# A graph attention layer and a routed expert layer on one core: four instruction streams reordered, a register kept, two banks alternated

## The chip, the core and the metric

One core of a Trainium2 chip runs the whole kernel in one launch. The metric is the time of one execution on the device in microseconds; the number for a kernel is the median of its runs.

## The reference

`x` is 4096 x 256 in fp32, `adj` a symmetric 0/1 matrix of 4096 x 4096. The layer is a graph attention followed by a mixture of eight experts (two per row), each with a residual:

```python
xn = layernorm(x)
Wh = xn @ W
e  = leaky_relu(Wh @ a[:256] + (Wh @ a[256:]).T, 0.2)
e  = where(adj > 0 or diagonal, e, -9e15)
x  = x + softmax(e, axis=1) @ Wh
xt = layernorm(x)
probs = softmax(xt @ Wr + br)
top_p, top_idx = top_k(probs, 2); weights = top_p / top_p.sum()
xe = layernorm(xt) * ln_g[e] + ln_b[e]
y  = gelu(xe @ W1[e] + b1[e]) @ W2[e] + b2[e]
out = x + sum of the two chosen y, times their weights
```

## The kernel before

Five engine programs are written out by hand and meet in semaphores; nothing is scheduled by a tool. What stands in an engine's program is what it does, in that order.

**Head** (0 to 63 us). VectorE takes statistics of 32 row tiles of x (`next_stats`, `moments`), GpSimd turns variances into reciprocal roots (`scales`), VectorE and GpSimd normalise the tiles, TensorE transposes them in pairs and multiplies by `W` (`pair_t`, `pair_row`, `project`).

**Attention** (63 to 579 us). Step i treats row tile i against all 4096 columns. ScalarE masks the two halves of tile i + 2 (L966) and takes the exponentials of tile i + 1, also in two halves (L1021). TensorE transposes the probabilities in four groups (L776); ScalarE copies each group from PSUM (`p_hi`, L1029: the high parts of three groups and an fp32 copy of the fourth), VectorE makes the low parts (L1314); TensorE multiplies by `Wh` (`av`). Groups 0 and 2 share one PSUM buffer, 1 and 3 the other, so the transposes of group 1 of the next step wait for the copy of group 3. VectorE also makes the scores of tile i + 2 in halves (L1294) and adds mask and minimum (L1302). GpSimd and ScalarE split the expert weights on the side, one chunk a step: a subtraction (L559) and a scaling (`w_scaled`, L1050).

Four finished tiles are a router batch b, treated in the steps that follow; q is i modulo 4. At q = 1 ScalarE normalises the four tiles to rows (`normalise`, L1037); at q = 2 TensorE transposes them (L808), ScalarE copies (L1056), TensorE forms the logits (L819); at q = 3 VectorE finds the two experts and their one-hots (L1382 to L1386) and TensorE counts positions (`router_pos`, L827 to L831); at q = 0 VectorE reads them (`choose_rows`).

SP's queue runs in this order each step (`tile_step`): store a finished tile (L419), load the two halves of the next adjacency tile (L394, each when ScalarE has masked the half before), store and load weight chunks (L405, L401), load a tile of x again (L426). The last one waits for rows:

```python
def load_x1(n):
    if n >= XRING:
        sp.wait_ge(s_row, n - XRING + 1)
        sp.wait_ge(s_out, 16 * (n - XRING + 2))
    sp.dma_start(x1[n % XRING][:, :], x_view[:, n, :]).then_inc(s_xr[n % XRING], 16)
```

**Experts** (579 us to the end). 32 full tiles of 256 rows and 7 half tiles of 128 (from NB = 32 to FT = 39), each of one expert, whose number is read from a table at run time. For tile t TensorE does `up` of t + 1 (L901 to L903), the transposes of t + 2 (L879) and `down` of t (L919, L922) into the PSUM banks `acc`; VectorE splits x and h and forms the result (L1609 to L1617), GpSimd scatters it with an add into `out` (L665), one scatter after the other has landed. The first 12 tiles and those from 28 on are written out, the rest is a loop.

Of the kernel before, what the change touches and what calls it, by code (L numbers as in the profile page):

```python
# [22 lines left out]
def build(nc, x, adj, gnn_w, gnn_a, w_r, b_r, ln_g, ln_b, w1, b1, w2, b2, out):  # L23
# [61 lines left out]
    with ExitStack() as ctx:  # L85
# [253 lines left out]
        def halves(t):  # L339

            return S if not isinstance(t, int) or t < NB else 1

        def total(t, each):

# [349 lines left out]
        def _(pe):  # L694
# [139 lines left out]
            def attend(i):  # L834

                u, b, q = i % 2, i // RB - 1, i % RB
                now = i < T
                if now:
                    p_transpose(i, u, 0)
                    if i == 0:  # L840
                        project(NP - 1)
                    p_transpose(i, u, 1)
                if i > 0:
                    av(i - 1, 1 - u, 2)
                    av(i - 1, 1 - u, 3)
                if in_batch(b) and q == 2:
                    router_t(b, 0)
                if now:
                    p_transpose(i, u, 2)
                    av(i, u, 0)  # L850
                if in_batch(b) and q == 2:
                    router_mm(b, 0)
                    router_t(b, 1)
                if in_batch(b) and q == 3:
                    router_pos(b)
                if now:
                    p_transpose(i, u, 3)
                    av(i, u, 1)
                if in_batch(b) and q == 2:
                    router_mm(b, 1)  # L860

# [21 lines left out]
            def expert_of(t):  # L883
                return pe.value_load(table_e[0:1, bass.ds(t, 1)], min_val=0, max_val=E - 1)

            def up(t, first=0, last=HC):
                e = expert_of(t)
                if first == 0:
                    pe.wait_ge(s_wr, e * CHUNKS + CHUNKS)
                    pe.wait_ge(s_xh, t + 1)  # L890
# [14 lines left out]
                        m.then_inc(s_g1, 1)  # L905

            def down(t, u):
                e = expert_of(t)
                pe.wait_ge(s_hh, t + 1)
                if within(t, 1, FT):  # L910
                    pe.wait_ge(s_yc, total(t, 2))
                else:
                    pe.wait_ge(s_x1, X1 * (T - 1) + 3)
                ns = halves(t)
                for c in range(HC):
                    w_both = w_blocks[:, bass.ds(e * CHUNKS + 2 + c // 4, 1), :, (c % 4) * D:(c % 4 + 1) * D].rearrange("p a z n -> p (a z) n")
                    w_hi = w_both[:, 0, :]
                    for s in range(ns):
                        pe.matmul(acc[s][:, :], h_hi[u][:, (c * ns + s) * P:(c * ns + s + 1) * P], w_both,  # L919
                                  start=(c == 0), stop=False, skip_group_check=True)  # L920
                    for s in range(ns):
                        m = pe.matmul(acc[s][:, 0:D], h_lo[u][:, (c * ns + s) * P:(c * ns + s + 1) * P], w_hi,  # L922
                                      start=False, stop=(c == HC - 1), skip_group_check=True)
                m.then_inc(s_down, 1)

# [33 lines left out]
        def _(act):  # L959
# [129 lines left out]
            def attend(i):  # L1089
# [13 lines left out]
                if i < T - 1:  # L1103
                    exps(i + 1, 1 - u, 0)
                    exps(i + 1, 1 - u, 1)
                if in_batch(b) and q == 1:
                    for k in range(RB):
                        normalise(b, k)
                if in_batch(b) and q == 2:
                    router(b, 0)  # L1110
                if now:
                    p_hi(i, 2)
                    w_scaled(i)
                if ahead:
                    mask(i + 2, u, 1)
                if in_batch(b) and q == 2:
                    router(b, 1)
                if now:
                    p_hi(i, 3)
                if i == T - 2:  # L1120
                    load_first()
                if in_batch(b) and q == 3:
# [79 lines left out]
        def _(dve):  # L1202
# [36 lines left out]

            next_stats(0, 4)  # L1240
            moments(0)
            next_stats(4, 8)
            moments(1)
            scaled_by(0)
            for i in range(4):
                normalise(i)
            next_stats(8, 12)
            scaled_by(1)
            normalise(4)
# [350 lines left out]
            def result(t, r):  # L1600

                e = dve.value_load(table_e[0:1, bass.ds(t, 1)], min_val=0, max_val=E - 1)
                ns = halves(t)
                y = y_sb[r % 2]
                dve.wait_ge(s_down, t + 1)
                if within(t, 2, FT):
                    dve.wait_ge(s_ysc, total(t - 1, 16))
                for s in range(ns):
                    dve.scalar_tensor_tensor(out=y[:, s, :], in0=acc[s][:, D:2 * D], scalar=1.0 / LOSCALE,  # L1609
                                             in1=b2_rep[:, bass.ds(e * D, D)], op0=ALU.mult, op1=ALU.add).then_inc(s_yc, 1)  # L1610
                dve.wait_ge(s_yc, total(t, 2) + ns)
                for s in range(ns):
                    dve.tensor_tensor(y[:, s, :], acc[s][:, 0:D], y[:, s, :], ALU.add).then_inc(s_yc, 1)
                dve.wait_ge(s_yc, total(t + 1, 2))
                dve.wait_ge(s_wt, t + 1)
                for s in range(ns):
                    ins = dve.tensor_scalar(y[:, s, :], y[:, s, :], weight[r][:, s:s + 1], None, ALU.mult)  # L1617
                ins.then_inc(s_y, 1)
# [68 lines left out]
```

## Time and profile before

| | us |
|---|---|
| median of 3 runs | 990.39 |
| range of the runs | 988.03 to 991.64 |
| profiled execution | 994.33 |
| its span | 992.4 |
| TensorE busy | 950.7 |
| VectorE busy | 788.8 |
| ScalarE busy | 615.4 |
| GpSimd busy | 622.0 |

The profiled execution is one run of its own; sums are made against it. In the rows PE is TensorE's matmuls, PEld its weight loads, DVE VectorE, ACT ScalarE, POOL GpSimd, SPq SP's DMA issues; L12 is a line of the kernel. Ends of matmuls are modelled, so idle time of PE is counted from a modelled end, some 0.16 us after the array is free for a transpose. What released a wait is inferred from semaphores. A wait named "issue" is one for nothing that the profile shows.

### The profile page before, as it was taken

What the parts mean: (1) busy time and instruction counts of PE and PEld (TensorE: products, weight loads), DVE (VectorE), ACT (ScalarE), POOL (GpSimd) and SP (SyncE); (2) the same over time, 40 slices, a digit from 0 to 9 for tenths busy, and PEclk for the clock granted to TensorE, in tenths of its full rate; (3) what the DMA queues carried; (4) which work ended last, traced back from release to release, by engine and by line L of the source; (5) the groups of instructions that cost most, each with busy time, mean ns of one, the idle gap of its engine ahead of it and who ended that gap; (6) DMA issues with size and microseconds to landing.
All of it is one profiled execution on the core that took longest, in us unless ns stands there. A gap on an engine that the chain in (4) does not pass through costs nothing. (4 is left out here: it accounts for less than half of the span.)

```text
span 992.4 us, 22974 instructions
## 1 busy us (share of the span) xinstructions
PE 950.7 (96%) x7562; PEld 799.7 (81%) x7563; DVE 788.8 (79%) x1199; ACT 615.4 (62%) x905; POOL 622.0 (63%) x630
## 2 busy tenths in 40 slices
PE   6999999999999999999999999999999999999994
PEld 5788999989988889888888977777777777777762
DVE  6789989999999999999999446787666666577653
ACT  4889898788888887878786554433333433333441
POOL 5221251486674964847629458888888888888652
PEclk9999999999999999999999999999999999999998
DMA  8658878688787787886877986443332332232321
GB/s 265 134 159 254 269 237 272 205 256 242 223 260 271 221 258 244 236 270 181 264 240 202 352 336 212 94 110 62 61 55 44 48 58 43 43 52 46 44 35 22
DMA packets 92636, 170.71 MB, mean 172 GB/s; under 512 B 20480, under 2 KB 69888, under 8 KB 84224
## 3 DMA queue, kind: packets, MB, share of 16 engines
q1 hardware_dynamic: 57984, 133.54, 40.3%
q0 software_dynamic: 24048, 26.23, 17.0%
q10 hardware_dynamic: 10512, 9.72, 3.4%
q8 instruction: 57, 0.93, 0.4%
q14 instruction: 35, 0.29, 0.1%
HBM read 136.65 MB, written 41.19 MB: 179 GB/s over the span
## 5 line engine op out<-in xcount | busy, mean ns | idle before, releaser
L1162 ACT ACTIVATE hf<-tp,b_cols 128x256 f32<-128x256 f32 (+1 forms) x312 | 116.4, 460 | 176.1 <-PE tp L903 173.7
L795 PE MATMUL acc<-wh,pt_hi 128*128 128x256 f16 x768 | 209.3, 273 | 0.0
L796 PE MATMUL acc<-wh,pt_hi 128*128 128x256 f16 x768 | 209.3, 273 | 0.0
L797 PE MATMUL acc<-wh,pt_lo 128*128 128x256 f16 x768 | 209.3, 273 | 0.0
L559 POOL TENSOR_TENSOR x_late<-x_late,wsp 128x1024 f32<-128x1024 f32 x32 | 78.9, 2464 | 178.2 <-DMA x_late<-in_L_ffn_W 173.0
L919 PE MATMUL acc<-w_sb,h_hi 128*128 x568 | 170.9, 379 | 5.1 <-issue 3.8
L1294 DVE SCALAR_TENSOR_TENSOR sc<-t_row,s_col 128x2048 f32<-128x2048 f32 x64 | 166.4, 2599 | 9.1 <-PE tp L776 6.9
L901 PE MATMUL tp<-x_hi,w_sb 128*128 128x256 f16 (+1 forms) x624 | 161.2, 264 | 1.9 <-ACT hf L1162 1.8
L665 POOL DMA_INDIRECT out<-y_sb,yidx x71 | 120.9, 1703 | 65.2 <-DVE y_sb L1617 38.1
L903 PE MATMUL tp<-x_down,w_sb 128*128 128x256 f16 (+1 forms) x624 | 161.2, 264 | 0.0
L902 PE MATMUL tp<-x_lo,w_sb 128*128 128x256 f16 (+1 forms) x624 | 160.8, 263 | 0.0
L1021 ACT ACTIVATE sc<-sc,mn 128x2048 f32<-128x2048 f32 x64 | 127.8, 2000 | 27.0 <-DVE mn L1302 26.9
L1302 DVE CUSTOM_DVE_ANT_0 sc<-sc,bias_sb 128x4096 f32<-128x4096 f32 x32 | 141.6, 4425 | 1.6 <-issue 0.2
L776 PE MATMUL tp<-ident,sc 128*128 128x128 f32 x1024 | 129.9, 274 | 9.4 <-ACT pt L1029 6.7
L599 POOL DMA_INDIRECT rows_dram<-rows,slot x64 | 118.0, 1844 | 23.2 <-issue 16.6
L1314 DVE SCALAR_TENSOR_TENSOR pt_lo<-tp,pt_hi 128x1024 f16<-128x1024 f32 x96 | 113.9, 1207 | 21.6 <-ACT pt_hi L1029 11.2
L1029 ACT ACTIVATE pt_hi<-tp 128x1024 f16<-128x1024 f32 x96 | 95.1, 1017 | 54.7 <-PE tp L776 50.0
L776 PEld LDWEIGHTS tp<-ident,sc 128*128 128x128 f32 x1024 | 114.6, 141 | 16.9 <-ACT pt L1029 8.3
L966 ACT ACTIVATE bias_sb<-adj_sb,big 128x2048 bf16<-128x2048 f32 x64 | 127.9, 1999 | 0.0
L1586 DVE CAST x_hi<-xg 128x512 f16<-128x512 f32 (+1 forms) x39 | 19.8, 508 | 123.9 <-ACT xg L1151 110.2
L799 PE MATMUL acc<-wh,pt 128*128 128x256 f32 x512 | 115.8, 379 | 0.0
L922 PE MATMUL acc<-w_sb,h_lo 128*128 x568 | 113.0, 273 | 0.0
(238 smaller groups left out, 1779.4 us busy)
## 6 DMA issues: line engine op xcount, KB each, us to landing
adj_sb<-in_adj SPq DMA_DIRECT2D x64, 1024.0 KB, 7.5
x_late<-in_L_ffn_W SPq DMA_DIRECT2D x32, 512.0 KB, 9.8
wsplit_dram<-wsp SPq DMA_DIRECT2D x32, 512.0 KB, 7.3
w_sb<-wsplit_dram SPq DMA_DIRECT2D x32, 512.0 KB, 8.7
xs<-rows_dram ACTq DMA_DIRECT2D x32, 260.0 KB, 3.4
wsp<-in_L_ffn_W POOLq DMA_DIRECT2D x32, 256.0 KB, 4.9
x<-in_x SPq DMA_DIRECT2D x32, 128.0 KB, 10.5
out<-x SPq DMA_DIRECT2D x32, 128.0 KB
```

The source lines that it names most:

```text
L776: m = pe.transpose(tp[g % 2][:, c * P:(c + 1) * P], sc[u][:, (GJ * g + c) * P:(GJ * g + c + 1) * P], ident[:, :])
L795: pe.matmul(o, pt_hi[g][:, cols], wh[:, j, 0, :], start=(j == 0), stop=False)
L796: pe.matmul(o, pt_hi[g][:, cols], wh[:, j, 1, :], start=False, stop=False)
L797: m = pe.matmul(o, pt_lo[g][:, cols], wh[:, j, 0, :], start=False, stop=False)
L901: pe.matmul(o, w_hi, x_hi[:, cols], start=(k == 0), stop=False)
L902: pe.matmul(o, w_hi, x_lo[:, cols], start=False, stop=False)
L903: m = pe.matmul(o, w_lo, x_down[:, cols], start=False, stop=(k == KD - 1))
L919: pe.matmul(acc[s][:, :], h_hi[u][:, (c * ns + s) * P:(c * ns + s + 1) * P], w_both, start=(c == 0), stop=False, skip_group_check=True)
L966: act.activation(bias_sb[u][:, cols], adj_sb[:, cols], ACT.Relu, bias=big[:, 0:1], scale=-3.0e38).then_inc(s_mk[h], 1)
L1021: act.activation(sc[u][:, cols], sc[u][:, cols], ACT.Exp, bias=mn[u][:, 0:1], scale=-1.0, accum_out=rsum[u][:, h:h + 1]).then_inc(s_e[h], 1)
L1294: dve.scalar_tensor_tensor(out=sc[u][:, cols], in0=t_row[:, cols], scalar=s_col8[:, bass.ds(n, 1)], in1=t2_row[:, cols], op0=ALU.add, op1= ...
L1302: dve.tensor_tensor_reduce(sc[u][:, :], sc[u][:, :], bias_sb[u][:, :], 1.0, 3.0e38, ALU.add, ALU.min, mn[u][:, 0:1]).then_inc(s_b, 1)
```

## The change

- VectorE, head: rows 0 and 1 are normalised right after the first four tiles' moments, ahead of the next four tiles' statistics.
- TensorE: `router_pos` goes behind the fourth group's transposes and the second product group of its step.
- ScalarE: `w_scaled` of each step, and the four rows of a q = 1 step, go behind the copy of the fourth group.
- TensorE, experts: where t is known when the program is written, `up` keeps the expert's register and `down` uses it.
- TensorE and VectorE, half tiles: odd and even tiles use different banks of `acc`, and `down` waits for the result two tiles back.

```diff
+        def bank_of(t):
+            return (t - NB) % 2 if isinstance(t, int) and t >= NB else 0
...
-                if in_batch(b) and q == 3:
-                    router_pos(b)
                 if now:
                     p_transpose(i, u, 3)
                     av(i, u, 1)
+                if in_batch(b) and q == 3:
+                    router_pos(b)
...
+            experts = {}
+
             def up(t, first=0, last=HC):
-                e = expert_of(t)
+                e = experts[t] if first > 0 else expert_of(t)
+                if isinstance(t, int):
+                    experts[t] = e
...
             def down(t, u):
-                e = expert_of(t)
+                e = experts.pop(t) if isinstance(t, int) and t in experts else expert_of(t)
+                a = bank_of(t)
                 pe.wait_ge(s_hh, t + 1)
-                if within(t, 1, FT):
+                if within(t, NB + 1, FT) and isinstance(t, int):
+                    pe.wait_ge(s_yc, total(t - 1, 2))
+                elif within(t, 1, FT):
                     pe.wait_ge(s_yc, total(t, 2))
...
-                        pe.matmul(acc[s][:, :], h_hi[u][:, (c * ns + s) * P:(c * ns + s + 1) * P], w_both,
+                        pe.matmul(acc[s + a][:, :], h_hi[u][:, (c * ns + s) * P:(c * ns + s + 1) * P], w_both,
...
-                if in_batch(b) and q == 1:
-                    for k in range(RB):
-                        normalise(b, k)
                 if in_batch(b) and q == 2:
                     router(b, 0)
                 if now:
                     p_hi(i, 2)
-                    w_scaled(i)
                 if ahead:
                     mask(i + 2, u, 1)
                 if in_batch(b) and q == 2:
                     router(b, 1)
                 if now:
                     p_hi(i, 3)
+                    w_scaled(i)
+                if in_batch(b) and q == 1:
+                    for k in range(RB):
+                        normalise(b, k)
...
             next_stats(0, 4)
             moments(0)
+            scaled_by(0)
+            normalise(0)
+            normalise(1)
             next_stats(4, 8)
             moments(1)
-            scaled_by(0)
-            for i in range(4):
-                normalise(i)
+            normalise(2)
+            normalise(3)
```

VectorE's `result` reads `acc[s + a]` in the same way.

On ScalarE, in step 5 (q = 1), the first with a router batch: `sc,rsum` are the exponentials, `rows` the normalised rows, `pt_hi` and `pt` the copies, `wsp` the scaling, `bias_sb` the mask. Before:

```order
L1021 ACTIVATE sc,rsum<-sc,mn 128x2048 [waits masked_with_min_done]
L1021 ACTIVATE sc,rsum<-sc,mn 128x2048
L1037 ACTIVATE rows<-x_0,nb,rs 128x256 [waits row_shift_done]
L1037 ACTIVATE rows<-x_1,nb,rs 128x256 [waits row_shift_done]
L1037 ACTIVATE rows<-x_2,nb,rs 128x256 [waits row_shift_done]
L1037 ACTIVATE rows<-x_3,nb,rs 128x256 [waits row_shift_done]
L1029 ACTIVATE pt_hi<-tp 128x1024 [waits av_done,p_transposed]
L1050 ACTIVATE wsp<-x_late 128x1024 [waits w_chunk_rest_done]
L966 ACTIVATE bias_sb<-adj_sb,big 128x2048 [waits masked_with_min_done,adj_half_loaded1]
L1029 ACTIVATE pt<-tp 128x1024 [waits av_done,p_transposed]
```

And with the change:

```order
L1032 ACTIVATE sc,rsum<-sc,mn 128x2048 [waits masked_with_min_done]
L1032 ACTIVATE sc,rsum<-sc,mn 128x2048
L1040 ACTIVATE pt_hi<-tp 128x1024 [waits av_done,p_transposed]
L977 ACTIVATE bias_sb<-adj_sb,big 128x2048 [waits masked_with_min_done,adj_half_loaded1]
L1040 ACTIVATE pt<-tp 128x1024 [waits av_done,p_transposed]
L1061 ACTIVATE wsp<-x_late 128x1024 [waits w_chunk_rest_done]
L1048 ACTIVATE rows<-x_0,nb,rs 128x256 [waits row_shift_done]
L1048 ACTIVATE rows<-x_1,nb,rs 128x256 [waits row_shift_done]
L1048 ACTIVATE rows<-x_2,nb,rs 128x256 [waits row_shift_done]
L1048 ACTIVATE rows<-x_3,nb,rs 128x256 [waits row_shift_done]
```

Third copy, mask and fourth copy now come right after the exponentials; scaling and rows come last.

On TensorE, before the down product of a half tile: the transposes of the tile after next, the register load and two register operations, and the product's first instruction with its waits. Before:

```order
L879 MATMUL xt_ps<-ident,xs 128x128 [waits ffn_xt_scaled,xs_loaded0]
L879 MATMUL xt_ps<-ident,xs 128x128
L884 TENSOR_LOAD table_e
L884 ISA x2
L919 ISA [waits ffn_y_low_added,ffn_hidden_split]
L919 MATMUL acc<-w_sb,h_hi 128x512
L922 MATMUL acc<-w_sb,h_lo 128x256
```

And with the change:

```order
L883 MATMUL xt_ps<-ident,xs 128x128 [waits ffn_xt_scaled,xs_loaded0]
L883 MATMUL xt_ps<-ident,xs 128x128
L930 ISA [waits ffn_y_low_added,ffn_hidden_split]
L930 MATMUL acc<-w_sb,h_hi 128x512
L933 MATMUL acc<-w_sb,h_lo 128x256
```

The load and the two register operations are gone there; the waits stay with the product's first instruction.

## Rows read from the trace of the kernel before

**Rows 1.** The page: busy time of the engines (share, instructions), and the group of scores

```profile
PE 950.7 (96%) x7562; PEld 799.7 (81%) x7563; DVE 788.8 (79%) x1199; ACT 615.4 (62%) x905; POOL 622.0 (63%) x630
...
L1294 DVE SCALAR_TENSOR_TENSOR sc<-t_row,s_col 128x2048 f32<-128x2048 f32 x64 | 166.4, 2599 | 9.1 <-PE tp L776 6.9
```

**Rows 2.** Waits, whole span: engine line waited for: us in total, times, longest

```profile
PE tp L776 <- ACT pt L1029: 6.7, 7, 1.3
...
PE rt_ps L827 <- DVE oh L1386: 4.9, 6, 1.2
...
PE acc L919 <- issue: 3.8, 7, 0.7
...
PE tp L776 <- DVE pt_lo L1314: 2.6, 8, 0.9
```

**Rows 3.** Windows, steps 21 to 24: length; busy PE, PEld, DVE, ACT, POOL; PEclk, DMA, GB/s

```profile
423.94:440.50 16.56, 15.41 (x136) 13.87 (x136) 16.36 (x30) 12.77 (x12) 8.99 (x5) 1.00 0.81 259
...
sum 65.49, PE 62.82 PEld 56.85 DVE 62.90 ACT 53.42 POOL 42.21; mean PE 15.70 PEld 14.21 DVE 15.73 ACT 13.36 POOL 10.55
```

**Rows 4.** Timeline, DVE and POOL: start, length, engine, line, operation, [idle before <-releaser]

```profile
372.89 2.35 DVE L1294 SCALAR_TENSOR_TENSOR sc<-t_row,s_col 128x2048 f32<-128x2048 f32 x1 [0.17 <-PE tp L776]
...
403.27 1.23 DVE L1314 SCALAR_TENSOR_TENSOR pt_lo<-tp,pt_hi 128x1024 f16<-128x1024 f32 x1 [1.36 <-issue]
404.41 4.34 DVE L1294 SCALAR_TENSOR_TENSOR sc<-t_row,s_col 128x2048 f32<-128x2048 f32 x1
...
404.43 2.16 POOL L559 TENSOR_TENSOR x_late<-x_late,wsp 128x1024 f32<-128x1024 f32 x1
```

**Rows 5.** Timeline, ScalarE, step 21 (q = 1) and the one behind it

```profile
396.29 2.00 ACT L1021 ACTIVATE sc<-sc,mn 128x2048 f32<-128x2048 f32 x1 [1.56 <-DVE mn L1302]
...
400.27 2.06 ACT L1037 ACTIVATE rows<-x,nb,rs 128x256 f32<-128x256 f32 x4
...
404.09 1.99 ACT L966 ACTIVATE bias_sb<-adj_sb,big 128x2048 bf16<-128x2048 f32 x1
405.99 1.00 ACT L1029 ACTIVATE pt<-tp 128x1024 f32<-128x1024 f32 x1
...
409.09 1.99 ACT L966 ACTIVATE bias_sb<-adj_sb,big 128x2048 bf16<-128x2048 f32 x1
...
417.51 0.57 ACT L1056 ACTIVATE xnt_b<-xt_ps 128x512 f32<-128x512 f32 x1
```

**Rows 6.** Timeline, PE, steps 21 and 22

```profile
407.04 1.09 PE L776 MATMUL tp<-ident,sc 128*128 128x128 f32 x8 [1.33 <-ACT pt L1029]
...
418.35 0.96 PE L819 MATMUL rt_ps<-w_r_sb,xnt_b 128*128 128x8 f32 x8
```

**Rows 7.** Timeline, SP's queue, step 21

```profile
400.88 0.33 SPq L426 DMA_DIRECT2D x<-in_x  x1
...
402.15 4.29 SPq L394 DMA_DIRECT2D adj_sb<-in_adj  x2
```

**Rows 8.** One tile, adj_sb: its transfers

```profile
DMA to landing us min/median/max: 5.8/7.5/11.7
```

**Rows 9.** One line (L884), PEld's queue: us of one, from to; and PEld's timeline, tail

```profile
L884 PEldq TENSOR_LOAD <-table_e x79: 295/303/782, 575.5 to 975.3; - x79
L884 PEldq SEQ_ASSERT  x79: 18/18/26, 576.3 to 976.1; - x79
...
946.15 0.10 PEld L919 LDWEIGHTS acc<-w_sb,h_hi 128*128 128x128 f16 x1 [0.78 <-issue]
```

**Rows 10.** Timeline, PE and POOL, the last tile

```profile
978.42 0.39 PE L919 MATMUL acc<-w_sb,h_hi 128*128 x1 [1.30 <-DVE y_sb L1613]
...
983.87 1.56 POOL L665 DMA_INDIRECT out<-y_sb,yidx  x1 [2.98 <-DMA out<-y_sb,yidx]
```

**Rows 11.** Timeline, PE, head

```profile
10.62 1.11 PE L720 MATMUL tp<-ident,rows 128*128 128x128 f32 x4 [2.07 <-DVE rows L1221]
...
30.99 0.63 PE L720 MATMUL tp<-ident,rows 128*128 128x128 f32 x4 [0.33 <-DVE sc L1221]
```

More of the change, by code:

```diff
@@ L918, in down @@
                     for s in range(ns):
-                        pe.matmul(acc[s][:, :], h_hi[u][:, (c * ns + s) * P:(c * ns + s + 1) * P], w_both,
+                        pe.matmul(acc[s + a][:, :], h_hi[u][:, (c * ns + s) * P:(c * ns + s + 1) * P], w_both,
                                   start=(c == 0), stop=False, skip_group_check=True)
                     for s in range(ns):
-                        m = pe.matmul(acc[s][:, 0:D], h_lo[u][:, (c * ns + s) * P:(c * ns + s + 1) * P], w_hi,
+                        m = pe.matmul(acc[s + a][:, 0:D], h_lo[u][:, (c * ns + s) * P:(c * ns + s + 1) * P], w_hi,
                                       start=False, stop=(c == HC - 1), skip_group_check=True)
@@ L1603, in result @@
                 ns = halves(t)
+                a = bank_of(t)
                 y = y_sb[r % 2]
@@ L1608, in result @@
                 for s in range(ns):
-                    dve.scalar_tensor_tensor(out=y[:, s, :], in0=acc[s][:, D:2 * D], scalar=1.0 / LOSCALE,
+                    dve.scalar_tensor_tensor(out=y[:, s, :], in0=acc[s + a][:, D:2 * D], scalar=1.0 / LOSCALE,
                                              in1=b2_rep[:, bass.ds(e * D, D)], op0=ALU.mult, op1=ALU.add).then_inc(s_yc, 1)
@@ L1612, in result @@
                 for s in range(ns):
-                    dve.tensor_tensor(y[:, s, :], acc[s][:, 0:D], y[:, s, :], ALU.add).then_inc(s_yc, 1)
+                    dve.tensor_tensor(y[:, s, :], acc[s + a][:, 0:D], y[:, s, :], ALU.add).then_inc(s_yc, 1)
                 dve.wait_ge(s_yc, total(t + 1, 2))
```

## The prediction

> **What bounds the kernel now.** TensorE first: it is busy for 950.7 of 992.4 us [rows 1], so only its stalls can be won. The list of its waits, read next, says where they are [rows 2]: seven for ScalarE's copy of the fourth group (6.7 us), six for the one-hots (4.9), eight for VectorE's low parts (2.6), all in the attention, and seven "issue" stalls before the down products (3.8).
>
> Then the four windows of one router batch, steps 21 to 24 (q = 1, 2, 3, 0) [rows 3]. TensorE idles for 2.7 of their 65.49 us, so this looks like TensorE's kernel. But VectorE is busy for 62.90 us of them, no less than TensorE's 62.82. The two run in lock step: a stall taken from TensorE is won only if idle time of VectorE goes with it. VectorE's timeline shows how little it has [rows 4]: 1.36 us before a low part that waited for the copy of the third group (the q = 1 steps but the first have it), and 0.17 before scores that waited for TensorE's fourth transposes in the third step.
>
> **The move on ScalarE, at first sight.** In a q = 1 step the exponentials end at 400.27. Four rows (2.06 us), the third copy and the weight scaling (together to 404.09) and a mask (1.9) stand ahead of the fourth copy at 405.99 [rows 5], which TensorE's next transposes await until 407.04 [rows 6]. With rows and scaling behind it, that copy starts at 403.1 and TensorE's wait is gone; the third copy starts at 400.3, and VectorE's 1.36 us are gone too. If that were all, each batch would be 1.4 us shorter.
>
> **What is queued behind the rows.** Completion of the first row lets SP load an x tile (`load_x1` waits for row n - 5), and behind that load, in SP's order, stands the load of an adjacency half. SP sits until 400.88, just after the first row, and issues the half at 402.15 [rows 7], 1.9 us after the row's start. ScalarE masks the half at 409.09 and hadn't to wait for it [rows 5], so it took at most 6.9 us; the shortest load of the trace took 5.8 [rows 8]. That is about 1 us of slack, and the change moves the first row by two copies and the scaling (1.85 for copy and scaling, 0.9 for the other copy) and the mask (1.9): 4.65 us. The mask of the q = 2 step will wait for its DMA, and with it all that ScalarE has behind it.
>
> How far that reaches, counted from the start of the q = 1 exponentials: exponentials 4.0, copy 0.9, mask 1.9, copy 0.9, scaling 0.95 make 8.65; from row to load issue 1.6 (1.9 here, less where SP's store goes quicker); the load, L; then mask 2.0, two exponentials 4.0 and the router's copy 0.6, before TensorE may start the logits product. Together 16.85 + L. Now the same stretch is 396.29 to 418.35, 22.1 us [rows 5, 6]. With L = 5.8 the new one is 0.55 longer, with 6.9 it is 1.65 longer, with the median of 7.5 [rows 8] 2.25. I take L = 6.3: only two x tiles stand ahead of this half in its queue, which puts it near the minimum. That is +1.05 a batch, and from the logits product on, the fourth transposes, the scores and VectorE's saturated stretch follow as they do now. It occurs six times (q = 1 of steps 5 to 25): **+6.3 us**, bounds +3.3 and +13.5. VectorE's 1.36 us are lost inside this chain, which starts before them.
>
> The Trainium skill (DMA: Bandwidth & Descriptors, Anatomy of one DMA) prices a transfer at about 2.0 us plus bytes over 436 GB/s, an estimate of 4.4 us for this half. By that estimate the six batches would give 5 us back instead; the shortest load here, 5.8, speaks against it, and the sum doesn't use it.
>
> **The other parts.**
> - Step 29 is a q = 1 step with no mask left to load for. Its gain is real: VectorE's 1.36 us, up to the 1.8 that TensorE stalls there. **-1.5**.
> - Step 1: only the scaling moves behind the fourth copy. One of the seven waits [rows 2] is there, and the scaling is 0.95 us of it; VectorE isn't saturated yet. **-1.0**, bounds 0 and -1.0.
> - Position products (L827 to L831) behind the fourth transposes and a product group: TensorE comes to them 3.5 us later than now and finds the one-hots ready, so 4.9 us of waits go [rows 2]. VectorE still has all its work in the same order and wins only where it waited for those transposes: 0.17 once [rows 4], some more in others. **-0.9**, bounds 0 and -4.9; I stand near zero because VectorE is busy for 16.36 of the 16.56 us of this very step [rows 3]. `choose_rows` reads the positions in the next step and isn't held up.
> - Kept register. In the tail (half tiles) TensorE's sequencer has no lead. Before a down product it loads the expert from the table (303 ns) and works on it until the assertion, from 975.3 to 976.1 [rows 9], and the weight loads stand for 0.78 us [rows 9]. There are seven such places, the tiles from 31 on but the last; I take 0.67 each, between 0.3 (the load alone) and 0.78. **-4.7**, bounds -2.1 and -5.5. In full tiles no such wait shows, and nothing is won. The chain that ends last runs through the tail, so it counts in full. What would be late next is VectorE's split of the next x; no wait for it is in [rows 2].
> - Alternating banks: `down` then waits for the result before the previous one. Only the last tile waits for that now, 1.30 us [rows 10]. But the last scatter, at 983.87, waits for the one before it to land, not for its data [rows 10]. **0**, bounds 0 and -0.4.
> - Head: rows 0 and 1 normalised before the second statistics. TensorE can start some 1.6 us before 10.62 [rows 11]. Then it meets VectorE, whose work is neither less nor earlier: at 30.99 it already waits for it [rows 11]. **0**, bounds +0.1 and -1.6.
>
> **Sum**: 6.3 - 1.5 - 1.0 - 0.9 - 4.7 = -1.8 us. The profiled execution took 994.33 (span 992.4), 3.9 above the median of the runs; its own time would become 992.5, and the median of 990.39 becomes **988.6**. About 0.5%, 5 us, is what a measurement of this kernel tells from no change: the forecast is no change, two sides that nearly cancel.
>
> **Rivals.**
> - *The late mask costs nothing*: something covers the logits product, and six batches keep VectorE's 1.36: -8.2 in place of +6.3, sum -16.3, 974. For: no wait of that product is in [rows 2]. Against: the copy that it reads ends within 0.3 us of its start (417.51 + 0.57 against 418.35 [rows 5, 6]). Chance 0.17.
> - *VectorE and GpSimd stand in each other's way less.* At 404.41 scores take 4.34 us, while GpSimd's subtraction runs from 404.43 for 2.16 [rows 4]; all 64 scores average 2.60 us [rows 1] where an undisturbed one takes 2.35 [rows 4], 16 us in all. The change moves their phases. In q = 1 steps the scores would start first, at 403.1, but except in step 29 that falls inside the chain that waits for the mask. In other steps a shift of either sign is open; a third of the 16 us won is -6, sum -7.8, 982.6. Chance 0.13. The Trainium skill (SBUF — State Buffer, SBUF: two separate sides) has the rule that whichever of the two starts first holds the shared ports for its whole instruction; by that rule step 29 gains 2 us more for VectorE, and the sum there goes to the 1.8 of TensorE.
> - *Slower: the half lands late.* Now it is alone in its queue for 4 us; afterwards the second half, free long before, is issued right behind it. If the two share, L is somewhere between 5.8 and the longest load, 11.7 [rows 8]; halfway, 8.8, costs 2.5 us more in six batches, sum +13.2, 1003.6. It decides from L = 7.4 on, where the sum passes +5. For: no row here shows a half with another right behind it and the queue empty. Against: the 6.9 of the half that was issued with a store beside it. Chance 0.12.
> - *The register load isn't what the tail waits for*, and its stalls stay with the semaphores: sum +2.9, 993.3. Chance 0.06.
>
> The forecast has 0.52; of it 0.07 lies below 985.4 and 0.01 above 995.4. With the rivals: **faster 0.31, same 0.57, slower 0.12**. The range for 8 in 10 is **979 to 995**: it takes in the lesser contention and the load up to 7.4, and leaves out the first and the third rival. The forecast's own is 985 to 993.
>
> **What would show it.** In step 21's place the half is issued some 4.7 us later against the exponentials, and the q = 2 mask waits for adj_sb, six times 3 to 4 us. Of TensorE's waits those for the fourth copy and the one-hots are gone; in their place, six times, stands one of the logits product (L819) for the router's copy, 2 to 3 us. The "issue" stalls of the tail are near zero, its tiles 0.7 us closer together. The last scatter still waits for the one before. The forecast falls if L819 doesn't wait, if VectorE's idle time in a batch is under 1 us, or if the tail's stalls only change their name.

## The result, and the profile after

| | before | changed |
|---|---|---|
| median, us | 991.9 (8 runs) | 1000.44 (8 runs) |
| range | 988.03 to 994.30 | 998.73 to 1003.85 |
| profiled execution, its span | 994.33, 992.4 | 999.58, 997.6 |

The ratio is 1.0094 (95% interval 1.008 to 1.0108): slower by 0.9%, 9 us, and outside the range. The forecast was 988.6. The profiled executions are only 5.2 us apart in span: that of before, 994.33, lies at the upper end of its kernel's runs, that of the change, 999.58, near the lower end of its own. So places are found in the traces, and sizes are judged by the ratios.

In the account below, "the minimum" is VectorE's instruction that adds the mask and finds the minimum, "the subtraction" is GpSimd's on the expert weights, and two instructions "meet" when they run at the same time. Busy times and two of VectorE's groups on the page after (scores, and the minimum):

```profile
PE 956.7 (96%) x7562; PEld 803.7 (81%) x7563; DVE 794.6 (80%) x1199; ACT 615.3 (62%) x905; POOL 631.9 (63%) x630
...
L1307 DVE SCALAR_TENSOR_TENSOR sc<-t_row,s_col 128x2048 f32<-128x2048 f32 x64 | 164.0, 2562 | 8.7 <-PE tp L780 6.7
...
L1315 DVE CUSTOM_DVE_ANT_0 sc<-sc,bias_sb 128x4096 f32<-128x4096 f32 x32 | 154.4, 4825 | 1.6 <-issue 0.2
```

VectorE is 5.8 us busier than in [rows 1]. The scores lost 2.4 us, but the minimum took 4.42 us every time before (32 times, 141.6 us), and here it takes 12.8 more in all.

The waits (engine, tile and line waited for; us in total, times, longest):

```profile
ACT bias_sb L977 <- DMA adj_sb<-in_adj: 22.4, 6, 3.9
...
PE rt_ps L823 <- ACT xnt_b L1067: 8.7, 6, 1.7
PE tp L780 <- DVE pt_lo L1327: 7.9, 14, 1.1
```

The waits for the fourth copy and for the one-hots of [rows 2] are gone, as forecast. In their place stand six waits of the mask for the adjacency tile, 3.7 us on average (forecast 3 to 4), and six of the logits product for the router's copy, as forecast, but of 0.8 to 1.7 us and not 2 to 3. The windows of steps 21 to 24, as in [rows 3]:

```profile
396.84:412.05 15.21, 15.02 (x120) 13.49 (x121) 15.09 (x14) 12.15 (x11) 13.86 (x14) 1.00 0.50 147
412.05:433.81 21.76, 19.46 (x146) 17.25 (x145) 18.73 (x17) 15.91 (x18) 13.86 (x8) 0.92 0.93 283
433.81:449.01 15.20, 15.20 (x136) 13.91 (x136) 15.06 (x30) 12.77 (x12) 10.88 (x6) 1.00 0.81 244
449.01:463.86 14.85, 14.85 (x127) 13.57 (x124) 14.61 (x22) 12.58 (x11) 3.28 (x4) 1.00 0.76 248
sum 67.02, PE 64.54 PEld 58.23 DVE 63.49 ACT 53.41 POOL 41.88; mean PE 16.13 PEld 14.56 DVE 15.87 ACT 13.35 POOL 10.47
```

The batch takes 67.02 us, was 65.49: the q = 3 step is 1.36 shorter, the q = 2 step 2.46 longer, and in that step TensorE is *busy* for 1.68 us more with the same work. Its clock column says why: 0.92. Inside it:

```profile
426.46:427.84 1.38, 1.38 (x12) 1.38 (x13) 0.50 (x1) 1.38 (x2) 0.00 (x0) 1.00 1.05 371
427.84:431.30 3.46, 3.46 (x19) 2.91 (x18) 2.25 (x2) 3.38 (x4) 2.19 (x2) 0.51 1.10 385
431.30:433.80 2.50, 2.50 (x25) 2.33 (x24) 2.45 (x4) 0.44 (x1) 2.19 (x2) 1.00 0.86 249
```

For 3.46 us behind the wait of the logits product the granted clock is 0.51, the lower of its two levels (1.2 in place of 2.4 GHz). It happens in three of the six batches (from 294.7, 359.6 and 427.9 us, 3.4 us each); before the tail the trace of before has no such stretch. The Trainium skill ("TensorE: Matmul & The Clock Gate", What's actually happening) knows these two states and no level between; the trace agrees: products of 256 columns stand 109 ns apart at one level and 213 at the other. The length of the wait alone doesn't say whether the clock falls: the two longest waits of the logits product, 1.7 and 1.6 us in the first two batches, are followed by no such stretch, those of 1.6, 1.6 and 1.4 in the next three are.

The chain that was forecast, on ScalarE in steps 21 and 22 (the exponentials, the fourth copy, the rows, the mask, the router's copy), on SP's queue (x load, adjacency half, weight chunk), and on TensorE (logits, then the fourth transposes), in three views:

```profile
403.73 2.00 ACT L1032 ACTIVATE sc<-sc,mn 128x2048 f32<-128x2048 f32 x1 [1.96 <-DVE mn L1315]
...
410.51 1.01 ACT L1040 ACTIVATE pt<-tp 128x1024 f32<-128x1024 f32 x1
...
412.37 2.07 ACT L1048 ACTIVATE rows<-x,nb,rs 128x256 f32<-128x256 f32 x4
...
419.95 2.00 ACT L977 ACTIVATE bias_sb<-adj_sb,big 128x2048 bf16<-128x2048 f32 x1 [3.69 <-DMA adj_sb<-in_adj]
...
425.83 0.57 ACT L1067 ACTIVATE xnt_b<-xt_ps 128x512 f32<-128x512 f32 x1
```

```profile
412.99 0.33 SPq L430 DMA_DIRECT2D x<-in_x  x1
...
413.83 0.93 SPq L398 DMA_DIRECT2D adj_sb<-in_adj  x2
...
415.30 0.43 SPq L405 DMA_DIRECT2D x_late<-in_L_ffn_W  x1
```

```profile
426.46 1.06 PE L823 MATMUL rt_ps<-w_r_sb,xnt_b 128*128 128x8 f32 x8 [1.41 <-ACT xnt_b L1067]
...
427.84 1.89 PE L780 MATMUL tp<-ident,sc 128*128 128x128 f32 x8
```

The first row comes 8.64 us after the start of the exponentials (forecast 8.65), the half is issued 1.46 after it (1.6) and is there after 6.1 (6.3; 5.4 to 6.4 in the six batches, 6.0 on average); the logits product starts 22.73 after the exponentials, where it started 22.06 [rows 5, 6].

What was not forecast is on VectorE and GpSimd in step 22:

```profile
413.03 6.98 DVE L1315 CUSTOM_DVE_ANT_0 sc<-sc,bias_sb 128x4096 f32<-128x4096 f32 x1
...
429.77 3.61 DVE L1307 SCALAR_TENSOR_TENSOR sc<-t_row,s_col 128x2048 f32<-128x2048 f32 x1 [1.21 <-PE tp L780]
...
413.58 2.14 POOL L563 TENSOR_TENSOR x_late<-x_late,wsp 128x1024 f32<-128x1024 f32 x1
...
429.12 2.12 POOL L563 TENSOR_TENSOR x_late<-x_late,wsp 128x1024 f32<-128x1024 f32 x1 [6.96 <-DMA x_late<-in_L_ffn_W]
```

The second scores, 2.35 us before, take 3.61 beside GpSimd's subtraction. It runs there because its weight chunk is loaded behind the late adjacency half (issued at 415.30) and, as seen against the kernel with the rows put back (below), also takes longer: from the start of the exponentials to its issue 11.6 us for 9.8, from issue to subtraction 13.8 for 10.3. In the batches' q = 2 steps these scores take 2.35, 4.03, 3.51, 3.24, 3.61 and 4.23 us. The scores of q = 1 steps that took 4.34 [rows 4] take 2.34 now, but there the mask's wait covers them.

The Trainium skill ("SBUF — State Buffer", SBUF: two separate sides) lets whichever of VectorE and GpSimd starts first keep the shared ports for its whole instruction. The scores at 429.77 agree (second to start, 1.26 longer). The minimum doesn't: VectorE's 6.98 us, 2.56 more than usual, began at 413.03, and the subtraction at 413.58. Nor do the scores of [rows 4], which began 0.02 us ahead of the subtraction and took 4.34, while in the same trace scores at 173.13, 0.05 ahead, kept their 2.33 and the subtraction took 4.28. So the recorded starts alone don't tell which of the two waits; what does is open.

The tail, two of four half tiles of each kernel and the sum over the four, before:

```profile
939.10:946.20 7.10, 6.51 (x67) 4.78 (x68) 3.95 (x8) 3.16 (x12) 5.18 (x8) 1.00 0.42 58
946.20:953.10 6.90, 6.41 (x66) 4.76 (x67) 3.95 (x8) 2.99 (x11) 5.27 (x9) 1.00 0.24 38
...
sum 28.40, PE 26.25 PEld 19.29 DVE 15.87 ACT 12.48 POOL 17.83; mean PE 6.56 PEld 4.82 DVE 3.97 ACT 3.12 POOL 4.46
```

and after:

```profile
945.37:952.22 6.85, 6.79 (x69) 5.00 (x68) 4.00 (x8) 3.09 (x10) 4.76 (x7) 1.00 0.42 58
952.22:958.93 6.71, 6.71 (x68) 4.94 (x67) 3.95 (x8) 3.10 (x10) 4.97 (x7) 1.00 0.26 42
...
sum 27.31, PE 27.24 PEld 20.02 DVE 15.95 ACT 12.38 POOL 19.10; mean PE 6.81 PEld 5.00 DVE 3.99 ACT 3.09 POOL 4.77
```

The "issue" stalls before the down products are gone, but a tile is only 0.3 us shorter: TensorE's busy time rose from 26.25 to 27.24 in these four. In `up` the first products follow each other 56 ns apart, the later ones some 83 on average (every third one 124, the others 60 to 65); before, the first 21 to 24 of 48 went at 56, now 10 do (gaps of one tile's products in the two timelines). That TensorE's sequencer has lost its lead there is the likely reason, but no row shows it. The time won at the load is mostly given back there. The last scatter waits for the one before it as in [rows 10]:

```profile
989.09 1.56 POOL L669 DMA_INDIRECT out<-y_sb,yidx  x1 [3.07 <-DMA out<-y_sb,yidx]
```

### The profile page after: what moved, and what is told of

It is laid out like the page before. It is cut to its first block and busy times, and to the rows that moved or that the text cites. A ratio compares the mean times of both kernels' runs of the same rounds, so it can differ in the third digit from the quotient of the medians.

```text
span 997.6 us, 22905 instructions
## 1 busy us (share of the span) xinstructions
PE 956.7 (96%) x7562; PEld 803.7 (81%) x7563; DVE 794.6 (80%) x1199; ACT 615.3 (62%) x905; POOL 631.9 (63%) x630
## 5 line engine op out<-in xcount | busy, mean ns | idle before, releaser
L563 POOL TENSOR_TENSOR x_late<-x_late,wsp 128x1024 f32<-128x1024 f32 x32 | 83.5, 2610 | 175.7 <-DMA x_late<-in_L_ffn_W 169.2
L1307 DVE SCALAR_TENSOR_TENSOR sc<-t_row,s_col 128x2048 f32<-128x2048 f32 x64 | 164.0, 2562 | 8.7 <-PE tp L780 6.7
L1315 DVE CUSTOM_DVE_ANT_0 sc<-sc,bias_sb 128x4096 f32<-128x4096 f32 x32 | 154.4, 4825 | 1.6 <-issue 0.2
L977 ACT ACTIVATE bias_sb<-adj_sb,big 128x2048 bf16<-128x2048 f32 x64 | 128.0, 2000 | 22.4 <-DMA adj_sb<-in_adj 22.4
```

Of the source, the lines that this page charges most:

```text
L977: act.activation(bias_sb[u][:, cols], adj_sb[:, cols], ACT.Relu, bias=big[:, 0:1], scale=-3.0e38).then_inc(s_mk[h], 1)
L1307: dve.scalar_tensor_tensor(out=sc[u][:, cols], in0=t_row[:, cols], scalar=s_col8[:, bass.ds(n, 1)], in1=t2_row[:, cols], op0=ALU.add, op1= ...
L1315: dve.tensor_tensor_reduce(sc[u][:, :], sc[u][:, :], bias_sb[u][:, :], 1.0, 3.0e38, ALU.add, ALU.min, mn[u][:, 0:1]).then_inc(s_b, 1)
```

## The experiments

"Rows back" below means the changed kernel with the rows where they were. To place differences, six batches are cut at two points that the timelines show: from the start of the exponentials in a q = 1 step to the logits product of the next step (A), and from there to the next q = 1 step's exponentials (B). Each row is read from one trace, and that alone moves B by some 2.5 us, as before and "register alone" show, whose attention is the same. Sums over six batches, us:

| kernel | A | B | stretches at half clock |
|---|---|---|---|
| before | 132.95 | 257.31 | 0 |
| changed | 137.41 | 262.91 | 3 |
| rows back | 132.95 | 253.23 | 0 |
| rows alone | 138.82 | 263.95 | 4 |
| x load a tile later | 127.88 | 254.12 | 0 |
| filler of 14 / of 8 | 139.96 / 139.46 | 259.57 / 261.80 | 0 / 1 |
| positions alone | 132.92 | 257.29 | 0 |
| scaling alone | 132.95 | 251.81 | 0 |
| register alone | 132.94 | 254.81 | 0 |
| short subtraction, changed | 147.04 | 254.48 | 4, three of them 6.8 us |
| short subtraction, rows back | 130.62 | 242.76 | 0 |

### Rows back

```diff
+                if in_batch(b) and q == 1:
+                    for k in range(RB):
+                        normalise(b, k)
                 if in_batch(b) and q == 2:
                     router(b, 0)
...
                     w_scaled(i)
-                if in_batch(b) and q == 1:
-                    for k in range(RB):
-                        normalise(b, k)
```

> The changed kernel with the four rows of a q = 1 step back ahead of the third copy; everything else as changed. Theory A (the rows delay the load of the adjacency half; the q = 2 mask waits, TensorE waits at the logits product, and its granted clock falls to half three times behind such a wait): these batches cost 10.1 us of the two profiles' difference, so this kernel comes out near 987, some 5 us under the kernel before: what stays is step 1 (-1.0), the tail (-2.6), the head (-0.4) and a little from the positions. Theory B (the cost comes from the position products or the scaling in their new places, or from VectorE's minimum meeting GpSimd's subtraction, 12.8 us more in that group): it stays at 995 or above. A also says: no wait for adj_sb in the list of waits, no stretch at half clock before the tail.

Measured 986.99 (5 runs), ratio to before 0.9958 (0.9944 to 0.9971): theory A to the microsecond. The windows of its steps 21 to 24, the sum:

```profile
sum 64.29, PE 62.78 PEld 56.93 DVE 61.76 ACT 53.38 POOL 44.88; mean PE 15.69 PEld 14.23 DVE 15.44 ACT 13.35 POOL 11.22
```

and its wait for the half:

```profile
ACT bias_sb L977 <- DMA adj_sb<-in_adj: 0.3, 1, 0.3
```

The move of the rows is worth +13.5 us (1.0094 - 0.9958 of 991); everything else in the change makes it 4 us faster. In the table the rows are +4.5 in A and +9.7 in B, less 0.9 in steps 29 and 30.

### Rows alone

```diff
-                if in_batch(b) and q == 1:
-                    for k in range(RB):
-                        normalise(b, k)
...
                 if now:
                     p_hi(i, 3)
+                if in_batch(b) and q == 1:
+                    for k in range(RB):
+                        normalise(b, k)
```

> The kernel before with one edit: the four rows of a q = 1 step behind the fourth group's copy. Theory A: the delay of the first row is the same 4.65 us as in the changed kernel, so the six batches cost about 10 us and step 29 gives back 1: some 1001, six waits of the mask for adj_sb of 3 to 4 us, six waits of the logits product, and some stretches at half clock. Theory B: within 3 us of the kernel before.

Measured 1006.98 (5 runs), ratio 1.0174 (1.0154 to 1.0194): 17 us, more than the 10 expected.

```profile
ACT bias_sb L966 <- DMA adj_sb<-in_adj: 24.0, 6, 4.5
...
PE rt_ps L819 <- ACT xnt_b L1056: 9.8, 6, 2.2
PE rt_ps L827 <- DVE oh L1386: 7.6, 6, 2.4
```

Six waits of each kind, as in the change, and four stretches at half clock. The edit alone makes the loss; it takes no second edit. It costs even more than in company (17.3 us for 13.5): here TensorE waits 7.6 us for the one-hots, where the kernel before waited 4.9 and the change, with the position products moved, not at all.

### The load of x behind the halves

```diff
                 load_w(e, q)
-                load_x1(i)
+                if i > 0:
+                    load_x1(i - 1)
...
+            load_x1(T - 1)
             store_w(T - 3)
```

> The changed kernel, but SP issues the load of x tile n - 1 where it issued that of tile n, so the load that waits for the first row stands behind both adjacency halves of that step instead of ahead of them. Theory A: mask and logits product don't wait, the clock stays at 1.00, and the batches keep the earlier copies: VectorE's 1.36 us a batch in five of them. 10.1 of loss gone and 5 to 7 won: 982 to 985, median near 983. Rival within A (something else, such as VectorE's saturated stretch, takes the gain): 987. Theory B: it stays near 1000.

Measured 981.25 (4 runs), ratio 0.9901 (0.9885 to 0.9916): 10 us faster than before and 19 faster than the change. SP's queue, then ScalarE with VectorE's minimum:

```profile
389.56 8.88 SPq L398 DMA_DIRECT2D adj_sb<-in_adj  x2
...
400.46 0.33 SPq L430 DMA_DIRECT2D x<-in_x  x1
...
405.64 9.60 SPq L398 DMA_DIRECT2D adj_sb<-in_adj  x2
```

```profile
399.84 2.07 ACT L1050 ACTIVATE rows<-x,nb,rs 128x256 f32<-128x256 f32 x4
...
403.62 2.00 ACT L979 ACTIVATE bias_sb<-adj_sb,big 128x2048 bf16<-128x2048 f32 x1
...
411.52 0.57 ACT L1069 ACTIVATE xnt_b<-xt_ps 128x512 f32<-128x512 f32 x1
...
400.50 6.98 DVE L1317 CUSTOM_DVE_ANT_0 sc<-sc,bias_sb 128x4096 f32<-128x4096 f32 x1
```

The first half is issued at 389.56, ten us ahead of the first row at 399.84; the load that waits for that row comes at 400.46. The mask doesn't wait. The next exponentials wait for the minimum instead, 6.98 us beside the subtraction (1.91 us of wait in step 22). So the rows' place on ScalarE costs nothing by itself in this kernel: all of its loss goes through SP's order.

### The same load in the kernel before

The same diff on the kernel before.

> The kernel before with SP's load of x tile n - 1 where that of tile n was. Theory A: in the kernel before the half comes in time by 0.6 to 1.8 us, so nothing waits for it, and freeing it wins nothing: same as before within 0.3%. Rival (SP's order alone, by another spread of the DMA load, makes the version with this edit fast, not the rows' earlier copies): 3 us or more faster.

Measured 993.25 (10 runs), ratio 0.9999 (0.9981 to 1.0016): same. SP's order wins nothing where the half is in time.

### TensorE kept busy while it waits

```diff
             def router_mm(b, h):
-                pe.wait_ge(s_xlt, 2 * b + h + 1)
                 if b > 0:
                     pe.wait_ge(s_slot, b)
+                if h == 0 and b < NBATCH - 1:
+                    for j in range(14):
+                        pe.matmul(rt_ps[:, 128:128 + D], wh[:, j, 0, 0:P], wh[:, j, 0, :], start=True, stop=True)
+                pe.wait_ge(s_xlt, 2 * b + h + 1)
```

> The changed kernel with 14 products of 256 columns (109 ns each, 1.5 us) that TensorE does ahead of its wait for the first logits product of each q = 2 step; their result is never read. Theory A1 (the idle wait is what lets the granted clock fall, and the half clock costs 1.7 us each of three times): the waits of the logits product (1.0 to 1.9 us) are filled, no stretch at half clock, about 5 us faster than the changed kernel, 995. Rival (the clock falls for another reason, or its fall costs nothing on the path): same as the changed kernel or up to 2 us slower, 1000 to 1002.

Measured 1000.53 (5 runs), ratio 1.0099 (1.0082 to 1.0116): same as the change. Its waits:

```profile
ACT bias_sb L980 <- DMA adj_sb<-in_adj: 24.8, 6, 4.8
...
PE rt_ps L826 <- ACT xnt_b L1070: 2.0, 4, 0.8
```

The logits' wait is filled but for 2.0 us and no stretch at half clock is left, so in this trace, without the idle wait, the clock didn't fall. B fell by 3.3 us, but A rose by 2.6 and step 30, which had no wait to fill, took 1.4 more. A second form, `b < NBATCH - 2` and `range(8)`:

> The changed kernel with 8 products of 256 columns (0.87 us) ahead of the wait for the first logits product, in the six q = 2 steps whose wait was 1.0 to 1.9 us, so that they fit inside it; their result is never read. If the half clock costs on the path what the trace of the changed kernel shows for the second scores (0.4, 1.5 and 0.9 us late in three batches) and the longer filler lost its win through products that didn't fit (1.5 us in the last batch, 2.5 in the other six): no stretch at half clock and 2 to 3 us faster than the changed kernel, 997.5. If eight products are too few to keep the clock, or the loss lies elsewhere: 1000.4.

Measured 1000.36 (6 runs), ratio 1.0078 (1.0052 to 1.0105). One stretch at half clock was left; the second scores met the subtraction in three batches, 3.99, 4.23 and 4.15 us, and scores of another step took 4.25. Neither filler shows a gain that can be measured. But the test isn't clean. The adjacency halves took 6.2 and 6.4 us on average in these two traces, for 6.0 in that of the change, and in the longer form they were also issued 0.2 later; over six batches that is all that A rose by (2.6 and 2.1). What the fallen clock costs at the end is therefore open between 0 and 3 us, though in the trace of the change it made the second scores 0.4, 1.5 and 0.9 us late.

### Positions alone

```diff
-                if in_batch(b) and q == 3:
-                    router_pos(b)
                 if now:
                     p_transpose(i, u, 3)
                     av(i, u, 1)
+                if in_batch(b) and q == 3:
+                    router_pos(b)
```

> The kernel before with one edit: the position products behind the fourth transposes and the second product group. Theory P (TensorE's wait for the one-hots is won as a whole, since VectorE has 2.6 us of idle time in a batch to take the shift up): q = 3 steps of 15.2 us in place of 15.6 to 16.6, four to five us in the six batches, 986 to 987. Rival V, which the prediction held (VectorE bounds this stretch, so only its own idle time before the scores is won): 990, not to be told from the kernel before.

Measured 992.03 (12 runs) beside 993.15, ratio 0.9988 (0.9973 to 1.0004): the rival, which is the prediction's reading. The q = 3 steps of the six batches are 6.1 us shorter (91.2 from 97.3 in all), the q = 0 steps 2.6 longer, the q = 1 steps 1.9 and the q = 2 steps 1.7 (starts of the first transposes): all given back. (Against the trace with only the register kept, below, whose attention is that of before, it is 5.3 shorter and 7.7 longer.)

### Scaling alone

```diff
                     p_hi(i, 2)
-                    w_scaled(i)
...
                     p_hi(i, 3)
+                    w_scaled(i)
```

> The kernel before with one edit: the weight scaling of every step behind the fourth group's copy. Step 1 gains 0.95. In a q = 1 step the fourth copy comes 0.95 us earlier, and the first row, which stays ahead, doesn't move, so the adjacency half is not late. Theory: -1 to -3, 988 to 990. Rival (the scaling's later end delays GpSimd's subtraction into VectorE's long instructions, since one of the two holds up the other): no gain, or 1 to 2 slower.

Measured 988.47 (8 runs), ratio 0.9954 (0.9938 to 0.9971): -4.6 us, more than expected. A is as before; the gain is 5.5 in B and 0.95 in step 1. The two comparisons that make the one-hots (q = 3), before:

```profile
L1382 DVE TENSOR_TENSOR oh<-iota_e,idxf 128x32 f32<-128x32 f32 x8 | 5.3, 660 | 0.2
...
L1383 DVE TENSOR_TENSOR oh<-iota_e,idxf 128x32 f32<-128x32 f32 x8 | 3.4, 424 | 0.0
```

and here:

```profile
L1382 DVE TENSOR_TENSOR oh<-iota_e,idxf 128x32 f32<-128x32 f32 x8 | 1.5, 192 | 0.2
...
L1383 DVE TENSOR_TENSOR oh<-iota_e,idxf 128x32 f32<-128x32 f32 x8 | 1.5, 184 | 0.0
```

They had met the subtraction: in the trace of before, at 434.11, a comparison that alone takes 0.19 us took 2.12 beside a subtraction that began at 434.05. In these traces 5.7 us of VectorE are gone from just the work that TensorE's position products wait for, and those waits fell from 4.9 to 1.4 us. Part of this is the trace: all three one-hot operations together take 10.2 us in that of before, but 8.3 in two others with the same order on ScalarE (register alone, and the later load of x in the kernel before), and 4.5 here. Why the move of the scaling shifts the subtraction is not traced.

### Register alone

The two hunks on `experts` of the change, on the kernel before, without the second bank.

> The kernel before with one edit: the expert's register is kept from up to down. Theory S (the tail's 0.65 to 0.8 us stalls are the register load, but TensorE is held there by the supply of its instructions as well, so that up runs slower after a down without the stall): the down products' waits are gone and the tail ends 2.5 us earlier than before, 988.5. Rival (the whole 4.7 are won when the banks' wait is not changed with it): 986. In both the attention is as in the kernel before.

Measured 989.50 (10 runs), ratio 0.9967 (0.9948 to 0.9985): -3.3 us. From the down product of tile 31 to that of the last tile it takes 50.5 us, the kernel before 53.2 and the changed one 50.4: -2.6, near the number of theory S. Its reason, that the supply of instructions holds TensorE there, is argued from the gaps, not shown.

### A short subtraction beside VectorE

The subtraction works on 128 of its 1024 columns; the rest of the low parts of the expert weights is left out.

```diff
-                pool.tensor_tensor(wf[q], wf[q], wsp[q][:, 0:CW], ALU.subtract).then_inc(s_wp, 1)
+                pool.tensor_tensor(wf[q][:, 0:P], wf[q][:, 0:P], wsp[q][:, 0:P], ALU.subtract).then_inc(s_wp, 1)
```

> The changed kernel with GpSimd's subtraction of the weight chunks cut from 1024 to 128 columns (the low parts of the expert weights are then wrong for the rest; nothing else changes in what runs when). It stands beside short_rows_back, the same cut in the kernel with the rows put back; without the cut the two are 13.4 us apart. Theory L (the late half costs what it costs; in the kernel with the rows back the same subtraction holds up the scores of the q = 1 steps, on the path as well, 0.9 us a batch, so that without any collision the two kernels win alike): both 8 to 14 us faster, still 12 to 14 apart; this one near 990. Theory M (6.9 of the 13.4 are the subtraction's move into the second scores of the q = 2 steps): the difference falls to 6 or 7, and this one gains 7 more than the other.

> The changed kernel with the rows of q = 1 steps back ahead of the third copy, and the same cut of GpSimd's subtraction to 128 columns. Theory L: near 976 to 978, 12 to 14 below short_after. Theory M: near 983, 6 or 7 below it.

Measured 1001.96 (4 runs; ratio 1.0094, 1.0057 to 1.0132) and 973.00 (4 runs; 0.98, 0.9768 to 0.9831). Neither theory: the difference didn't stay or halve, it doubled, to 29 us. A q = 2 step and the sum over its batch, with the late half:

```profile
214.20:237.89 23.69, 20.91 (x147) 18.71 (x145) 16.27 (x17) 15.15 (x17) 9.55 (x8) 0.86 0.95 281
...
sum 68.54, PE 65.76 PEld 59.72 DVE 58.06 ACT 53.72 POOL 31.97; mean PE 16.44 PEld 14.93 DVE 14.52 ACT 13.43 POOL 7.99
```

and with the rows back:

```profile
209.80:227.14 17.34, 17.34 (x146) 16.06 (x145) 15.26 (x17) 14.44 (x14) 9.91 (x8) 1.00 1.05 326
...
sum 62.19, PE 62.19 PEld 57.07 DVE 57.72 ACT 53.62 POOL 34.20; mean PE 15.55 PEld 14.27 DVE 14.43 ACT 13.41 POOL 8.55
```

Without meetings the kernel with the rows back runs every batch in 62.2 us. The one with the late half gains nothing: the mask waits for the half longer than before (27.9 us in six waits, up to 5.6, for 22.4), and TensorE's clock is at half for 6.8 us in three q = 2 steps (0.86 over the whole step). Three things differ from the real kernel at once. The first row comes 9.5 us after the exponentials on average, where it was 8.8; the halves take 5.8 to 8.0 us, 7.0 on average, for 6.0, and why isn't known; and the clock: TensorE is busy for 13.3 us more than with the rows back (960.3 and 947.0), with the same 7562 products, which is nearly half of the 29. In the pair with the whole subtraction it was 5.3 of 12.3 us of span (956.7 and 951.4). So the pair shows that the late half costs time without the subtraction's meetings, and even more of it. What the meetings cost in the real kernel it doesn't show.

### Positions back in the fast version

> The fast version (the changed kernel with SP's load of x a tile later) with the position products back ahead of the fourth transposes. Alone they won nothing in the batches (-6 us in q = 3 steps, given back in the next three). If that holds here too: 981 to 983, not to be told from the fast version. Rival (with VectorE relieved, the wait for the one-hots is on the path): 4 to 6 us slower, 986.

The edit is the positions' diff, turned round, on the version with the later load. Measured 985.14 (6 runs), ratio 0.9921 (0.9896 to 0.9947), against 0.9901 (0.9885 to 0.9916): some 2 us slower, within the intervals. The medians themselves are 3.9 us apart, but they come from different sets of runs, in which the kernel before differed by 3.0 as well. The positions' place may be worth 2 us there, less than the rival's 4 to 6; it isn't shown.

## Why the prediction was wrong

- **The late half: right in every link up to the logits product, wrong in where it ended.** First row +8.64 for 8.65, load 5.4 to 6.4 us for 6.3, logits product 22.9 after the exponentials on average for 23.15, six waits of each kind, those of the logits product 0.8 to 1.7 us for 2 to 3. Stretch A grew by 4.5, where +6.3 was taken. The step that failed is the sentence that from the logits product on everything follows as now. B grew by 9.7 against the kernel with the rows back. In the trace the second scores of the q = 2 steps, which met the subtraction, since its chunk's load is queued on SP behind the late half as well, took 6.9 us more (20.97 in six, 14.1 undisturbed), and three of them started 2.8 later in sum, at half clock. The two make up the 9.7, but only in sum: the first batch lost 1.3 us in B with no meeting, the second 0.9 with scores 1.7 longer. That B lost it is shown; its division is argued, and the short subtraction speaks against it, since there B differs by 11.7 with next to no meetings. The prediction followed SP's queue only as far as the adjacency half, and had the fall of the clock in no rival. The term was +6.3 - 1.5 for six batches and step 29; the rows are worth +13.5, and steps 29 and 30 gave 0.9 in place of 1.5. The estimate of 4.4 us for the half, which the sum left out, was not met by any of the six (5.4 to 6.4). The Trainium skill (DMA: Bandwidth & Descriptors, Anatomy of one DMA) gives that fit for transfers that GpSimd issues, and this one is issued by SP.
- **Scaling**: -1.0 was taken for step 1 (0.95 in the trace) and nothing for the rest. Alone it is worth -4.6. The rival of lesser contention had a mechanism of this kind, with 0.13, but looked for it at the scores, which shrank by 2.4 us, and not at the one-hots.
- **Positions**: -0.9 forecast, -1.2 measured alone (-2.7 to +0.4). That a stall taken from TensorE is won only with idle time of VectorE was right here: 6.1 us won in one step and given back in three.
- **Register**: -4.7 forecast, -3.3 measured (-5.2 to -1.5), 2.6 between the traces. The stalls went in full, but the products behind them didn't keep their pace, which the prediction didn't ask about.
- **Banks and head**: the last scatter still waits for the one before (3.07 us), so nothing speaks against the banks' 0. The attention starts at 62.59 us for 63.00, but kernels whose head is unchanged start between 61.9 and 63.3, so the head's 0 is neither shown nor refuted. Neither part was run alone.
- **The rival on the slower side** had the right sign and the wrong cause. It priced a load of 7.4 us and more; the load took 6.0. The slowdown came behind it.

Alone, the four parts sum to 17.3 - 4.6 - 1.2 - 3.3 = +8.2 us, beside +9.3 measured. The agreement is luck: scaling, positions and register sum to -9.1 alone, but with the rows back, banks and head included, the change is worth only -4.2 (-5.6 to -2.9), and the rows cost 17.3 alone and 13.5 in company. Both differences are clear of the noise and nearly cancel. So the parts do act on each other, or the banks or the head cost something; which, no run tells.

## What to carry to other kernels

When a step is moved later, follow every queue that its completion releases to the end, not to the first late transfer: here, in the trace, the half, then the weight chunk behind it, then GpSimd's subtraction, then VectorE's scores beside it. A load that waits for late work belongs behind the loads that don't; one load's place in SP's order turned a loss of 9 us into a gain of 10. And a stall that is taken from the engine with the longest list of waits says little until it is known whose idle time pays for it.

## What had not been expected of the hardware

- TensorE's granted clock fell to half for 3.4 us behind waits of 1.4 to 1.6 us, in three of six batches, and not behind the two longest, 1.6 and 1.7, and for 6.8 us behind the longer waits without the subtraction (15.4 us in six, up to 3.5). With 14 products in the wait it stayed at 1.00; with 8 one stretch was left.
- The minimum with mask, started 0.55 us ahead of a subtraction of 2.14 us, took 6.98 in place of 4.42, in five of five such meetings of the changed kernel: VectorE can lose although it began first. Begun 3.3 us ahead of a subtraction (245.60 in the version with the later load), it kept its 4.43 and the subtraction took 3.10.
- In the tail the removal of a stall of 0.5 to 0.7 us a tile shortened the tile by only 0.2 to 0.3, since 11 to 14 of the products after it ran some 83 ns apart where they had run 56.
